# A decoder layer's local attention: the causal mask of the probability pass moves from TensorE matmuls to a selection on GpSimd

## What is computed

```python
qc, kc, vc = ...                              # b, heads, chunks, 64, 8
k_prev = concatenate([zero, kc[:, :, :-1]])   # the chunk before; zeros for chunk 0
kcat = concatenate([k_prev, kc], axis=3)      # 128 keys for 64 queries
scores = einsum('bhcqd,bhckd->bhcqk', qc, kcat) / HD ** 0.5
causal = wq[:, None] + W >= jk[None, :]       # key index <= query index + 64
valid  = ci[:, None, None] * W + jk - W >= 0  # chunk 0 has no chunk before it
scores = where(causal & valid, scores, -inf)
out = softmax(scores) @ vcat
```

## Time and profile before

| | |
|---|---|
| median of 3 runs | 502.47 us (501.01 to 503.45) |
| span of the profiled execution | 500.3 us |
| median less span | 2.2 us |
| PE busy | 378.0 us, 76% of the span |
| DVE busy | 306.0 us, 61% |
| ACT busy | 206.4 us, 41% |
| POOL busy | 182.3 us, 36% |
| mean granted TensorE clock | 0.943 of full speed |

### The profile page before, as it was taken

The page is one execution under the profiler, slowest core; times in us unless marked ns, Lnnn a source line. Parts: engine busy times, 40 slices in busy tenths (PEclk is TensorE's granted clock), DMA queues, the critical chain, the costliest instruction groups (busy, mean ns, idle before and its releaser), DMA issues. The chain is left out here.

```text
span 500.3 us, 11670 instructions
## 1 busy us (share of the span) xinstructions
PE 378.0 (76%) x4246; PEld 254.0 (51%) x4246; DVE 306.0 (61%) x680; ACT 206.4 (41%) x298; POOL 182.3 (36%) x265
## 2 busy tenths in 40 slices
PE   0146889899899897346887888879788783988794
PEld 0144557667667665232445454544545432766672
DVE  6285666566575661136777676768667513587875
ACT  1011344535544533221456566565656561222220
POOL 8262250440431530153141505233150305765652
PEclk9999899999999998857699999999999996999997
DMA  8300000000000000000000000000000000000000
GB/s 239 97 0 2 2 3 3 3 4 0 1 0 1 1 0 2 1 0 1 1 1 3 1 3 1 0 1 0 1 1 0 1 1 1 0 22 11 21 10 21
DMA packets 8138, 5.73 MB, mean 11 GB/s; under 512 B 1200, under 2 KB 7344, under 8 KB 8112
## 3 DMA queue, kind: packets, MB, share of 16 engines
q1 hardware_dynamic: 6768, 4.07, 3.0%
q10 hardware_dynamic: 1344, 1.31, 0.8%
HBM read 4.20 MB, written 1.05 MB: 10 GB/s over the span
## 5 line engine op out<-in xcount | busy, mean ns | idle before, releaser
L728 DVE TENSOR_REDUCE negm<-ps 128x2 bf16<-128x512 f32 (+1 forms) x192 | 123.6, 685 | 23.9 <-PE ps L386 16.9
L611 ACT ACTIVATE probs<-ps 128x1024 f32<-128x1024 f32 x96 | 98.0, 1025 | 48.4 <-PE ps L411 27.8
L837 POOL TENSOR_SCALAR q_stack<-rest 128x512 bf16<-128x512 f32 x18 | 27.8, 1545 | 92.2 <-DVE rest L692 92.2
L376 PE MATMUL ps<-KT,QT 128*128 128x256 bf16 x256 | 47.7, 289 | 13.0 <-DVE negm L728 11.9
L947 PE MATMUL ps<-xqT,tapw 128*128 128x256 f32 x198 | 49.1, 393 | 2.7 <-ACT xqT L1014 2.7
L596 ACT COPY QT<-ps 64x1024 bf16<-64x1024 bf16 x32 | 32.2, 1005 | 41.9 <-PE ps L342 41.9
L342 PE MATMUL ps<-identb,q_stack 128*128 128x128 bf16 x256 | 22.1, 236 | 34.7 <-ACT o_sb L618 10.8
L706 DVE COPY QT<-ps 64x1024 bf16<-64x1024 bf16 x32 | 22.2, 694 | 35.2 <-PE ps L342 35.1
L947 PEld LDWEIGHTS ps<-xqT,tapw 128*128 128x128 f32 x198 | 36.9, 196 | 9.0 <-ACT hid L1020 2.5
L376 PEld LDWEIGHTS ps<-KT,QT 128*128 128x128 bf16 x256 | 18.7, 99 | 44.2 <-DVE negm L728 40.3
L832 POOL TENSOR_TENSOR k_stack<-ones,mask_t 128x32 bf16<-128x32 f32 x9 | 4.0, 447 | 100.5 <-DVE rest L692 100.5
(11 more groups left out here) (154 smaller groups left out, 728.7 us busy)
## 6 DMA issues: line engine op xcount, KB each, us to landing
X<-in_x_dram SPq DMA_DIRECT2D x2, 512.0 KB, 7.3
out_dram<-ob SPq DMA_DIRECT2D x8, 128.0 KB, 1.8
cwb<-in_L_ffn_conv_w_dram ACTq DMA_DIRECT2D x1, 768.0 KB, 8.6
w_sb<-in_L_ffn_w_dram ACTq DMA_DIRECT2D x2, 256.0 KB, 5.9
QT<-mT SPq DMA_DIRECT2D x32, 4.0 KB
wqkv_sb<-in_L_attn_w_qkv_dram SPq DMA_DIRECT2D x1, 192.0 KB, 8.8
wout_sb<-in_L_attn_w_out_dram SPq DMA_DIRECT2D x1, 64.0 KB, 8.2
wraw<-in_L_xattn_Wq_dram SPq DMA_DIRECT2D x1, 64.0 KB, 7.9
```

Source lines behind the costliest of these rows:

```text
L376: last = nc.tensor.matmul(mb[:, u * S:(u + 1) * S], QT[:, p, pr, j, t * P:(t + 1) * P], KT[:, p, pr, W:W + S], start=True, stop=True)
L611: nc.scalar.activation(probs[:, g, :], ps[:, k:k + 2, :].rearrange("p a n -> p (a n)"), ACT.Exp, scale=SCALE).then_inc(s_exp, 1)
L728: nc.vector.tensor_reduce(o, src, AX.X, ALU.max, negate=True).then_inc(m_max, 1)
L837: nc.gpsimd.tensor_scalar(slots(stack, *mid), repeated(rest[:, i], mid[2]), 1.0, None, ALU.mult).then_inc(mid_done, 1)
```

## The change

The identity matmuls (L414) go away, and the score matmuls each start their own result. ScalarE takes the exp of the unmasked scores. GpSimd then sets the masked probabilities to zero with `affine_select`, in place, on 128 partitions x 1024 f32 per chunk, and `pv` waits for that (`s_kept`) and no longer for the exp. Chunk 0 has no chunk before it: its exp leaves out the lower 64 partitions, which VectorE zeroes once, in front of its first `x_stats`. GpSimd's order becomes: `normalise(b+2)`, the selections of chunks 0 and 1, `split(b+2)`, the selections of chunks 2 and 3. The mask of the maxima pass stays as it is.

```diff
+        s_zero = sem("no_previous_chunk")
...
-                            nc.tensor.matmul(o, identb[:], mask_k[:, min(g, 1):min(g, 1) + 1, :].to_broadcast([P, 8, W]),
-                                             start=True, stop=False, skip_group_check=True)
                             for u in range(4):
                                 pr = 4 * i + u
                                 last = nc.tensor.matmul(o[:, u * 2 * W:(u + 1) * 2 * W],
                                                         KT[:, p, pr, W * g:W * g + P],
                                                         QT[:, p, pr, :, W * g:W * g + W],
-                                                        start=False, stop=(u == 3), skip_group_check=True)
+                                                        start=True, stop=True)
...
-                        pe.wait_ge(s_exp, NS * b + i + 1)
+                        pe.wait_ge(s_kept, NS * b + i + 1)
...
-                    nc.scalar.activation(probs[:, g, :], ps[:, k:k + 2, :].rearrange("p a n -> p (a n)"), ACT.Exp,
+                    lo = 0 if cross or g else W
+                    if not cross and isinstance(b, int) and b == 0 and g == 0:
+                        act.wait_ge(s_zero, 1)
+                    nc.scalar.activation(probs[lo:P, g, :], ps[lo:P, k:k + 2, :].rearrange("p a n -> p (a n)"), ACT.Exp,
                                          scale=SCALE).then_inc(s_exp, 1)
...
+                if not cross:
+                    nc.vector.memset(probs[0:W, 0, :], 0.0).then_inc(s_zero, 1)
                 x_stats(0, 0)
...
+                def keep(b, g_):
+
+                    wait_apart(g, (s_exp, NS * b + g_ + 1))
+                    cur = probs[:, g_, :].rearrange("p (h q) -> p h q", q=W)
+                    nc.gpsimd.affine_select(out=cur, in_=cur, compare_op=ALU.is_ge, fill=0.0, base=W,
+                                            pattern=[[0, H], [1, W]], channel_multiplier=-1).then_inc(s_kept, 1)
+
+                def ahead(b, p, nxt):
+                    if nxt:
+                        normalise(b + 2, p)
+                    if not cross:
+                        keep(b, 0)
+                        keep(b, 1)
+                    if nxt:
+                        split(b + 2)
+                    if not cross:
+                        keep(b, 2)
+                        keep(b, 3)
...
                 with g.Fori(0, (B - 2) // 2) as k:
-                    normalise(2 * k + 3, 1)
-                    split(2 * k + 3)
-                    normalise(2 * k + 4, 0)
-                    split(2 * k + 4)
+                    ahead(2 * k + 1, 1, True)
+                    ahead(2 * k + 2, 0, True)
+                ahead(B - 1, 1, False)
```

More of the change, by code:

```diff
@@ L286, in attention @@
             mT_ps, mT_sb, m_row = sem(n + "max_turned"), sem(n + "max_copied"), sem(n + "max_rows")
-            s_ps, s_exp = sem(n + "scores"), sem(n + "probs")
+            s_ps, s_exp, s_kept = sem(n + "scores"), sem(n + "probs"), sem(n + "probs_masked")
             pv_ps, o_done = sem(n + "pv"), sem(n + "o_copied")
@@ L846, in pool_program @@
                 normalise(1, 1)
-                g_steps(g, normalise, split)
-            def g_steps(g, normalise, split):
                 split(1)
-                normalise(2, 0)
-                split(2)
+                ahead(0, 0, True)
                 with g.Fori(0, (B - 2) // 2) as k:
-                    normalise(2 * k + 3, 1)
-                    split(2 * k + 3)
-                    normalise(2 * k + 4, 0)
-                    split(2 * k + 4)
+                    ahead(2 * k + 1, 1, True)
+                    ahead(2 * k + 2, 0, True)
+                ahead(B - 1, 1, False)
             def sync_program(sp):
```

## The result

The changed kernel takes 521.9 us (median of 4 runs, 518.8 to 524.9) against 501.8 us for the kernel before (four runs; the forecast started from the 502.47 of three): 1.041 times the time before, 95% interval 1.036 to 1.047. The forecast was 511 us in a range of 504 to 521. The direction and the two mechanisms came out; the size did not: +20 us in place of +8.5. The profiled execution is the slowest of the four runs, 524.9 us with a span of 522.6; what follows is read from it.

A forecast was written before the change was run, and what follows sets the result against it. TensorE's queue was taken to pace the step before, a loop through GpSimd after the change. 502.47 + 4.3 (loop, last steps and memset) + 4.3 (clock falls) = 511 us, range 504 to 521.

The forecast's parts named there:

- The loop: Local steps through GpSimd: period 17.60 + 2k, k one selection's time (1.1 us); 19.8 us against 19.13, 4.0 over steps 0 to 5.
- from `stack_turn` to the split 143.95 - 131.36 = 12.59 us, less 0.85: Part of each local step's period: four mask matmuls of scores 0 and 1 go, 4 x 0.21 = 0.85 us saved.
- The clock: TensorE's idleness drops the granted clock in five of steps 0 to 6, 0.85 us a fall: 4.3 us.
- I add 0.5 because the clock may come back later: Step 7 of the local block: 0.5 us added for less dense work, within that step's -0.8 us.
- the sum for steps 6 and 7: End of the local block: step 6 k - 0.97 = 0.1 us, step 7 -0.8 us.
- the upper bound for the clock, 12 us: Steps 0 to 6: seven falls with all 3.4 us of half clock on the path, 7 x 1.7 = 12 us.
- The memset: Prologue: VectorE's memset of 1024 columns in front of the first statistics, covered by nothing, +0.9 us.
- The hidden selections: Chunks 0 and 1 in each local step: two selections need 2.2 us, end before pv 0 and are hidden.
- B: Rival, chance 0.22: the GpSimd loop binds but the clock holds; 507 us, by k from 504.6 to 508.5.
- C: Rival, chance 0.16: a selection costs far more, 1.9 us giving 518 to 522 with falls, 3.0 us giving 533.
- D: Rival, chance 0.08: the change gains, since 2k per step is less than TensorE's 1.53 us; 499 at k = 0.55.
- E: Rival, chance 0.07: k near 0.8 to 0.9 us without falls, within 2.5 us of no change.

The follow-up runs named there:

- the filler kernel: Changed kernel plus 13 matmuls per step that compute nothing, in TensorE's idle time in steps 0 to 6: 510.4 us, 1.020 of the kernel before.
- The run with half the columns: Changed kernel with the selections of chunks 2 and 3 over 512 of the 1024 columns: median 511.4 us, 1.024 of the kernel before.

## Why the prediction was too low

**The loop: right in kind, its growth 0.44 us a step too small.** Selections 1147 ns (taken: 1100), 1.55 us from pv 3 to `stack_turn` (1.54), idleness 2.22 and 0.35 us (2.3 and 0.6) all came nearly as written. The wrong term is "from `stack_turn` to the split 143.95 - 131.36 = 12.59 us, less 0.85", with its reason, "the stretch is otherwise TensorE's own work one piece after another". The pieces of a step at full clock, in us (two values where alternate steps differ):

| kernel | split to pv 3 | pv 3 to `stack_turn` | `stack_turn` to split |
|---|---|---|---|
| before | 4.99 | 1.55 | 12.59, 12.72 |
| changed, with filler | 6.47 | 1.55 | 12.21, 12.36 |
| masks away, no selections | 4.13 | 1.55 | 12.21, 12.36 |
| only chunk 0 by selection | 4.99 | 1.55 | 12.57, 12.72 |

The stretch lost 0.37 us and not 0.85. `v_project` needs the second copy of QT, and it did so in the kernel before already; first its two lines, then the same two with only chunk 0 by selection:

```profile
133.72 1.00 ACT L596 COPY QT<-ps 64x1024 bf16<-64x1024 bf16 x1 [0.71 <-PE ps L342]
...
134.85 1.11 PE L359 MATMUL ps<-wqkv_sb,xnT 128*128 128x128 f32 x8
```

```profile
151.48 1.00 ACT L604 COPY QT<-ps 64x1024 bf16<-64x1024 bf16 x1 [0.71 <-PE ps L344]
...
152.61 1.15 PE L361 MATMUL ps<-wqkv_sb,xnT 128*128 128x128 f32 x8 [0.28 <-ACT QT L604]
```

The copy ends at 134.72 and at 152.48, and `v_project` starts 0.13 us behind it both times; without the masks of scores 0 TensorE stands still for 0.28 us ahead of it. In the filler kernel the start is 0.06 or 0.14 us behind the copy's end, in turn. So of the 0.43 us that I counted for scores 0, at most 0.07 could be gained, and this could have been read in the trace of before. With 0.48 us less gained, and with pv 3 at 6.47 us behind the split where the formula with k = 1.147 has 6.61, the period is 17.60 + 0.48 - 0.14 + 2k = 20.23 us, as measured in the steps of the kind that the earlier trace rows shows. Over six periods the growth was 6.6 us and not 4.0.

**The clock: right that it falls, wrong in what a fall costs and where.** I wrote "I take 0.85 us a fall: 5 x 0.85 = 4.3". In the profiled execution it was 8.5 us for six falls in the periods (130.4 less the 121.9 of the filler kernel). My price came from one half-clock stretch of 3.4 us; five of six lasted twice as long. Three of these began around pv 2 and ended just ahead of `v_project`, two began shortly ahead of `stack_turn` and ended past `v_project`'s start, so both pairs of `stack_turn` with their copies lay in all five. This is the largest wrong term. Step 7 was mis-sized more in proportion: "I add 0.5 because the clock may come back later". The stretch to cross-attention grew by 4.2 us. It is shown here for the changed kernel, the kernel before, and the one with filler in steps 0 to 6:

```profile
199.43:237.63 38.20, 22.12 (x340) 16.99 (x334) 8.31 (x23) 9.77 (x16) 13.60 (x16) 0.65 0.01 1
```

```profile
182.35:216.36 34.01, 20.79 (x353) 14.93 (x352) 8.14 (x23) 10.18 (x16) 6.87 (x11) 0.82 0.00 1
```

```profile
189.80:222.74 32.94, 19.72 (x353) 13.63 (x347) 8.13 (x23) 9.79 (x16) 13.61 (x17) 0.87 0.01 1
```

A mean granted clock of 0.65 over 38.20 us is some 27 us at half clock; before it is 12 us, with filler 9. The filler run needs 5.3 us less than the changed kernel here, and 1.1 less than the kernel before. That is near the -0.7 of the sum for steps 6 and 7, but the comparison is not free of the clock, since the kernel before had a fall in step 7 and the filler run had none. The 1.1 us at the start of cross-attention lie in a stretch with low clock too (0.70, before 0.72).

The clock's part of the prologue was not brought by the change. The run with half the columns executes the same instructions up to the third split. Its maxima matmuls are at the 0.39 us of full clock from 49.7 on, not from 57, and it takes 36.95 us from the first to the third split where the changed kernel's profiled execution takes 39.18: 2.2 us for the clock of this one execution. The column of the granted clock can't be used here ahead of its first fall: it shows 1.00 in the kernel before at 33.98 and 39.58, where eight transposes take 1.01 us in place of 0.61.

Adding up for the two profiled spans: loop 15.2 - 8.5 = 6.6 us, memset 0.8, clock in the periods 8.5, stretch to cross-attention 4.2, the rest of the prologue and the start of cross-attention 2.2; together 22.3. Predicted were 4.0, 0.9 and 4.3, and -0.7 for steps 6 and 7. What is neither loop nor memset is 14.9 us and lies above the upper bound for the clock, 12 us, which left out what lies outside steps 0 to 6. Only the clock's part in the periods is measured by an experiment that removes it; that the last 4.2 and 2.2 us are mostly the clock is read from the stretches.

The clock's part varies from run to run: the four runs of the changed kernel had a mean clock of 0.875 to 0.904 and took 524.9 to 518.8 us. The filler run's median is 9.2 us above the kernel before, and its profiled execution only 6.5. What falls in which run I can't say.

**The memset** was right: the first statistics start at 21.91 in place of 21.02. **The hidden selections** were right, down to their end before pv 0. **The rivals:** B's mechanism, the loop at full clock, is the first filler run, at 510 and not 507. C named 518 to 522, and 521.9 lies there, but by luck: its reason, a selection of 1.9 us or more, did not occur (1.147). D and E are out, k is not below 0.9.

The Trainium skill, page "GPSIMD Engine Reference", section "Performance pitfalls for Q7 kernels", gives 1.03 cycles an element for the unrolled compare-and-select body; 0.95 ns a column is 1.14 cycles at the 1.2 GHz that the same page states, so the trace agrees nearly, and not with 2.03. The same skill, page "TensorE: Matmul & The Clock Gate", section "HAM oscillation — how this bites in real kernels", has the clock fall in every iteration of a loop in which TensorE waits 3 to 5 us for a DMA. The trace agrees with the repetition, six falls in six steps, but here a gap of 2.22 us and two short ones behind it were enough.

## What to carry to other kernels

Moving work from the busiest engine to an idle one gains only as far as the idle engine's queue is free at that point of the step: here it was free for 11 us and then busy for just the 4 us in which two of the four selections became due, so with two or three of them the kernel is 1.0 and 1.4% faster, and with all four in that order 4% slower. Before counting what a removed instruction saves, look at the next instruction's second input; a wait that ends 0.1 us earlier takes over at once. And a wait of 2 us on TensorE costs more than 2 us: it can put the next 3 to 7 us at half clock, which filler matmuls in the gap avoided here.

## What the runs showed of the hardware

In the kernel before, the stretch around `o_copy` had gaps of 0.28, 0.89 and 0.65 us and never brought the clock down in six steps; with 2.22 and 0.35 us ahead of it, it fell in each; with a single 0.94 us, or with 1.73 us and half selections, in three of six. Once down in the local steps it stayed so for 3.4 to 10 us. Adding matmuls that compute nothing shortened the kernel by 2% in one case and by 0.6% in another. GpSimd's `affine_select` in place took 661 ns for 128 x 512 f32 and 1147 ns for 128 x 1024, and hardly slowed VectorE's work beside it: VectorE was busy for 11.76 us in a step before and for 11.92 after, and its 192 reductions took 685 ns each in both kernels.
